# Value copies and the attention residual moved from ScalarE to VectorE, in an adapter, attention and mixture-of-experts kernel

## What is computed

```python
# layer 0: adapter with an expert chosen per sequence, then a norm
x = layer_norm(up(expert(gelu(down(x)))) + x)
# layer 1: attention (16 heads of 16 features) and a feed-forward net
x = ln(x) * (1 + scale) + shift             # scale, shift per sequence, from the timestep
q, k, v = x @ Wq + bq, x @ Wk + bk, x @ Wv + bv
probs = softmax(mask(q @ k.T / 4 + attention_bias))
x = x + ((probs @ v) @ Wo + bo)             # the residual of this case
x = x + gelu2((ln(x) * g2 + beta2) @ W1 + b1) @ W2 + b2
# layer 2: pairs of features rotated by theta and phi of the sequence
# layer 3: norms, a style, then each token through 2 of 8 experts of width 1024
y = sum(gate[e] * (relu(h @ w1[e] + b1[e]) @ w2[e] + b2[e]) for e in top2(softmax(h @ router)))
out = x + y
```

## Time and profile before

| | us |
|---|---|
| median of 3 runs | 693.06 |
| lowest and highest run | 692.5 and 694.13 |
| the profiled execution | 692.5 |
| its span in the trace | 690.7 |
| TensorE busy (matmuls) | 553.9 (80%) |
| VectorE busy | 470.9 (68%) |
| ScalarE busy | 289.4 (42%) |
| GpSimd busy | 259.1 (38%) |

### The profile page before, as it was taken

The page is one execution under the profiler, slowest core; times in us unless marked ns, Lnnn a source line. Parts: engine busy times, 40 slices in busy tenths (PEclk is TensorE's granted clock), DMA queues, the critical chain, the costliest instruction groups (busy, mean ns, idle before and its releaser), DMA issues.

```text
span 690.7 us, 15770 instructions
## 1 busy us (share of the span) xinstructions
PE 553.9 (80%) x5032; PEld 414.4 (60%) x5033; DVE 470.9 (68%) x1284; ACT 289.4 (42%) x596; POOL 259.1 (38%) x161
## 2 busy tenths in 40 slices
PE   2618587999588798778966499999989999999992
PEld 1505365676466385663855347767767777777771
DVE  5581797799969979972699662886653646474651
ACT  1313643734444325345333241666464435353540
POOL 0723554718506636125771140212441313132222
PEclk9557779999898989989988689999999999999996
DMA  8623445303024433308424685783632322222220
GB/s 293 225 91 122 153 147 195 132 1 123 35 89 159 178 132 112 123 25 312 152 93 145 238 318 189 282 273 55 156 75 45 48 35 48 33 46 38 44 42 0
DMA packets 41177, 86.37 MB, mean 125 GB/s; under 512 B 7321, under 2 KB 31938, under 8 KB 37026
## 3 DMA queue, kind: packets, MB, share of 16 engines
q1 hardware_dynamic: 22896, 65.16, 26.9%
q0 software_dynamic: 7200, 8.60, 7.5%
q10 hardware_dynamic: 11026, 11.89, 5.7%
HBM read 57.10 MB, written 29.44 MB: 125 GB/s over the span
## 4 chain that ended last, share of the span: by engine, by line
PE 51%; DVE 26%; DMA 6%; issue 6%; ACT 5%; ACTq 2%; POOL 2%; SPq 0%; DVEq 0%; POOLq 0%
PE bank L1902 8%; PE bank L1727 6%; PE bank L1891 5%; PE bank L1736 4%; PE bank L1893 4%; PE bank L1892 4%; PE bank L1903 4%; DMA out_x<-x_kept,ids 4%; PE bank L1624 2%; PE bank L1691 2%; DMA stage<-in_moe_w 2%; PE bank L1707 2%; DVE stats L1040 2%; PE bank L1611 2%; DVE w_moe L1151 2%
## 5 line engine op out<-in xcount | busy, mean ns | idle before, releaser
L1891 PE MATMUL bank<-xs_f,w_moe 128*128 128x128 f16 x624 | 123.2, 221 | 13.4 <-ACT stage L869 6.1
L653 POOL DMA_INDIRECT out_x<-x_kept,ids x39 | 61.6, 1579 | 167.3 <-DVE x_kept L1493 98.0
L1893 PE MATMUL bank<-xs_f,w_moe 128*128 128x128 f16 x624 | 123.4, 221 | 0.0
L1892 PE MATMUL bank<-xs_f,w_moe 128*128 128x128 f16 x624 | 122.8, 220 | 0.0
L869 ACT ACTIVATE stage<-bank,cols 128x128 f32<-128x128 f32 x312 | 88.4, 375 | 79.9 <-PE bank L1893 39.0
L1891 PEld LDWEIGHTS bank<-xs_f,w_moe 128*128 x624 | 61.1, 98 | 50.4 <-issue 21.9
L1902 PE MATMUL bank<-w_moe,split 128*128 x208 | 79.3, 383 | 0.4
L605 POOL DMA_INDIRECT dispatched<-disp,slot x32 | 35.9, 1121 | 97.8 <-DVE disp L1251 54.5
L1007 DVE SCALAR_TENSOR_TENSOR split<-stage,split 128x2048 f16<-128x2048 f32 x16 | 42.4, 2650 | 34.3 <-ACT split L692 34.3
L1727 PE MATMUL bank<-w_moe 128*128 128x512 f32 x128 | 60.6, 634 | 3.1 <-ACT w_moe L753 3.1
L1892 PEld LDWEIGHTS bank<-xs_f,w_moe 128*128 x624 | 61.4, 98 | 2.8
(11 more groups left out here) (271 smaller groups left out, 1210.3 us busy)
## 6 DMA issues: line engine op xcount, KB each, us to landing
stage<-in_moe_w SPq DMA_DIRECT2D x16, 1024.0 KB, 8.5
w_split<-split SPq DMA_DIRECT2D x16, 1024.0 KB, 4.9
w_moe<-w_split SPq DMA_DIRECT2D x8, 2048.0 KB
w_moe<-in_bias SPq DMA_DIRECT2D x8, 1024.0 KB, 10.0
xs<-dispatched ACTq DMA_DIRECT2D x41, 130.0 KB
w_moe<-in_x_f SPq DMA_DIRECT2D x4, 512.0 KB, 5.9
w_moe<-in_x_t SPq DMA_DIRECT2D x4, 512.0 KB, 4.6
out_x<-x4b ACTq DMA_DIRECT2D x4, 512.0 KB, 3.6
```

The lines of the kernel that those rows point to most:

```text
L653: pool.indirect_dma_start(out=out[:, :], out_offset=bass.IndirectOffsetOnAxis(ap=ids[m][:, 0:1], axis=0), in_=ys[j], in_offset=None, bound ...
L1891: pe.matmul(o, hi, xs_f[j][:, k, :], start=(k == 0), stop=False)
L1892: pe.matmul(o, hi, xs_f[j][:, KD + k, :], start=False, stop=False)
L1893: mm = pe.matmul(o, lo, xs_f[j][:, k, :], start=False, stop=(k == KD - 1))
```

## The change

Four edits. The copy of bank 1 to `v_bd` moves from ScalarE to VectorE (`values` in both blocks; ScalarE keeps bank 0). `take_x2` leaves ScalarE; VectorE's new `residual` adds `bo`, now laid out as a row over all partitions, while it takes banks 6 and 7 to `x2`. `keep` no longer adds `bo` and is one instruction of 128 x 1024. And the parameter load of `b2` (128 KB) becomes one of `bo` and `b2` together (256 KB).

```diff
-            (b2, t["b2"].broadcast_to([P, D])), (w1, t["w1"].rearrange("(k p) n -> p k n", p=P)),
+            (biases, t["biases"].broadcast_to([P, 2, D])), (w1, t["w1"].rearrange("(k p) n -> p k n", p=P)),
...
             def values(c):
 
-                for half, ready in enumerate((v0_ready, v1_ready)):
-                    act.wait_ge(v_done.sem, v_done.of(c, half + 1))
-                    for s in range(2):
-                        act.activation(
-                            v_bd[64 * s:64 * s + 64, 4 * half:4 * half + 4, :, s, :].rearrange("p b j d -> p (b j) d"),
-                            bank[half][64 * s:64 * s + 64, :].rearrange("p (j d) -> p j d", d=HD),
-                            ACT.Copy).then_inc(ready.sem, 1)
+                act.wait_ge(v_done.sem, v_done.of(c, 1))
+                for s in range(2):
+                    act.activation(v_bd[64 * s:64 * s + 64, 0:4, :, s, :].rearrange("p b j d -> p (b j) d"),
+                                   bank[0][64 * s:64 * s + 64, :].rearrange("p (j d) -> p j d", d=HD),
+                                   ACT.Copy).then_inc(v0_ready.sem, 1)
 
             def keep(c):
 
                 act.wait_ge(x1_ready.sem, x1_ready.of(c, 2))
                 act.wait_ge(wo_done.sem, wo_done.of(c, 0))
-                for k in range(KD):
-                    ins = act.activation(x1_kept[:, k, :], x1[:, k, :], ACT.Identity, bias=bo[:, k:k + 1])
-                ins.then_inc(kept_ready.sem, 1)
-
-            def take_x2(c):
-
-                for g in range(2):
-                    act.wait_ge(wo_done.sem, wo_done.of(c, g + 1))
-                    act.activation(x2[:, 2 * g:2 * g + 2, :], bank[6 + g][:].rearrange("p (n d) -> p n d", d=D),
-                                   ACT.Copy).then_inc(x2_ready.sem, 1)
+                act.activation(x1_kept[:], x1[:], ACT.Copy).then_inc(kept_ready.sem, 1)
...
+                def values():
+
+                    dve.wait_ge(v_done.sem, v_done.of(c, 2))
+                    for s in range(2):
+                        dve.tensor_copy(v_bd[64 * s:64 * s + 64, 4:8, :, s, :].rearrange("p b j d -> p (b j) d"),
+                                        bank[1][64 * s:64 * s + 64, :].rearrange("p (j d) -> p j d", d=HD)
+                                        ).then_inc(v1_ready.sem, 1)
...
+                def residual():
+                    for g in range(2):
+                        dve.wait_ge(wo_done.sem, wo_done.of(c, g + 1))
+                        dve.tensor_tensor(x2[:, 2 * g:2 * g + 2, :], bank[6 + g][:].rearrange("p (n d) -> p n d", d=D),
+                                          bo[:].unsqueeze(1).broadcast_to([P, 2, D]), ALU.add).then_inc(x2_ready.sem, 1)
...
             split_low(0, 0)
+            values()
             scores(0)
...
             norms()
             stages = second_half(0)
-            norm2, *_ = stages
+            residual, norm2, *_ = stages
+            residual()
             scale_norm, *_ = attention(1)
             scale_norm()
             split_low(0, 3)
```

More of the change, by code:

```diff
@@ L174, in build @@
         iota_p, parity, freqs, angle, down_b = (col[n] for n in ("iota_p", "parity", "freqs", "angles", "down_b"))
-        b_ada, bq, bk, bv, bo, b1 = (col[n] for n in ("b_ada", "bq", "bk", "bv", "bo", "b1"))
+        b_ada, bq, bk, bv, b1 = (col[n] for n in ("b_ada", "bq", "bk", "bv", "b1"))
         g2, beta2, ln_g, ln_b = (col[n] for n in ("g2", "beta2", "ln_g", "ln_b"))
@@ L818, in _ @@
             context(0, 1)
-            take_x2(0)
             split_high(0, 3)
@@ L844, in _ @@
                 context(c + 1, 1)
-                take_x2(c + 1)
                 split_high(c + 1, 2)
@@ L1122, in sums @@
                         finish()
-                return scale_norm, scores, sums
+                return scale_norm, values, scores, sums
             def second_half(c):
                 vec, _ = stepper(second_step, c)
+                def residual():
[3 more added lines that the diff above has]
+                                          bo[:].unsqueeze(1).broadcast_to([P, 2, D]), ALU.add).then_inc(x2_ready.sem, 1)
                 def norm2():
@@ L1267, in accumulate @@
                                                  x4[:, 2 * g:2 * g + 2, :], ALU.mult, ALU.add).then_inc(acc_ready.sem, 1)
-                return (norm2, second_residual, rotate, norm3, style_stats, style_scale, style_apply, choose,
+                return (residual, norm2, second_residual, rotate, norm3, style_stats, style_scale, style_apply, choose,
                         token_gates, find_place, copy_gates, accumulate, fill_rows)
             hidden, residual, norms = adapter(0)
-            scale_norm, scores, sums = attention(0)
+            scale_norm, values, scores, sums = attention(0)
             step(dve.tensor_copy(time_f[:], time_i[:]))
@@ L1364, in _ @@
             for c in range(NCH - 1):
-                _, scores, sums = attention(c + 1)
-                (_, second_residual, rotate, norm3, style_stats, style_scale, style_apply, choose,
+                _, values, scores, sums = attention(c + 1)
+                (_, _, second_residual, rotate, norm3, style_stats, style_scale, style_apply, choose,
                  token_gates, find_place, copy_gates, accumulate, fill_rows) = stages
+                values()
                 if c + 2 < NCH:
@@ L2062 @@
         "w_ada": a["L1_cond_W_ada"], "w_qkv": np.concatenate([a["L1_cond_Wq"], a["L1_cond_Wk"], wv], 1),
-        "wo": a["L1_cond_Wo"], "b2": row(a["L1_cond_b2"]),
+        "wo": a["L1_cond_Wo"], "biases": np.stack([a["L1_cond_bo"], a["L1_cond_b2"]])[None],
         "w1": a["L1_cond_W1"], "w2": a["L1_cond_W2"], "subj_emb": a["L3_cond_subj_emb"],
```

9 lines of the change are left out of this document (5 added, 4 removed).

## The result

The changed kernel takes 698.55 us (median of 11 runs, 696.46 to 700.35), the kernel before on the same chip 693.84 (11 runs, 691.72 to 695.92). The ratio is 1.0075, with a 95% interval of 1.006 to 1.0089: slower by 4 to 6 us. The sign was forecast; the time, 696.1 with a range of 692.8 to 698.2, was too low.

A forecast was written before the change was run, and what follows sets the result against it. No engine is full; in the attention stage the chain of waits hops between engines. 0.15 + 2.8 + 0.1 = +3.05 us on 692.5 gave 695.55 for such an execution, 696.1 for the median; range 692.8 to 698.2.

The forecast's parts named there:

- The sign: Whole kernel: slower at 0.68, same at 0.27, faster at 0.05.
- Values on VectorE: Values copies moved to VectorE: +0.15 us in chunk 0, +0.1 in chunk 2, nothing in chunks 1 and 3.
- `x2` in chunks 1 to 3: VectorE's two additions of 0.68 us fit into its idle before the routing choice: zero.
- in chunk 0, +0.1: x2 additions between the norms and scale_norm of chunk 1: the second ends at 112.37, scale_norm began at 112.23; +0.1 us.
- The collision: VectorE's low split goes ahead of GpSimd's second shift half in chunk 1; queries start at 117.4 instead of 115.09, +2.3 us.
- The clock: TensorE's idle before chunk 1's queries grows to 4.9 us, its clock falls to 1.2 GHz: 1.6 us lost (0 to 2.1).
- What of it passes: Of TensorE's 3.9 us, +2.8 goes on: VectorE reads chunk 1's first score at 150.25 instead of 147.46.
- Behind it all is relative: After chunk 1's scores and rotation the +2.8 us goes on; weight loads, too, are issued when VectorE has split.
- last rival: TensorE also falls to the lower clock later, or mask additions shift into more small VectorE steps: 698.5 us; chance 0.10.
- a difference arising after 170 us: Check on the new profile: if the difference arises after 170 us, its reason is another than the forecast's.

The follow-up runs named there:

- values_only: The kernel before, with only the copy of the values' second bank moved to VectorE: 693.39 us, ratio 1.0.
- late_split: The changed kernel, with ScalarE waiting for both halves of x2 of chunk 0 before split_high(0, 3): 693.74 us, ratio 1.0017.
- warm_gap_short: early_split plus four matmuls with unused results on TensorE ahead of the queries of chunk 1: 696.87 us, ratio 1.0056.
- warm_turn3_short: early_split plus four matmuls with unused results ahead of the transposes of chunk 1 in the loop: 696.13 us, ratio 1.005.
- two_waits: The changed kernel, with VectorE waiting for both halves of GpSimd's shift before its low split, in chunks 0 and 1: 693.39 us, ratio 0.9986.
- early_split: The kernel before, with ScalarE doing split_high(0, 3) ahead of take_x2(0), nothing moved between engines: 699.5 us, ratio 1.0082.
- warm_gap: early_split plus nine matmuls with unused results on TensorE ahead of the queries of chunk 1: 698.57 us, ratio 1.0071.
- wait_for_shift: The changed kernel, with VectorE waiting for both halves of GpSimd's shift of chunk 1 before split_low(0, 3): 695.06 us, ratio 1.0025.
- warm_turn3: early_split plus seven matmuls with unused results ahead of the transposes of chunk 1 in the loop: 698.1 us, ratio 1.0053.
- warm_both: early_split plus four unused matmuls at each of two places, ahead of chunk 1's queries and its transposes in the loop: 695.94 us, ratio 1.0038.
- warm_before: The kernel before, with matmuls with unused results in TensorE's idle stretches of the attention stage: 687.17 us, ratio 0.9919.
- warm_before_wait: The kernel before, with VectorE's wait for the shift in chunk 0 and unused matmuls in TensorE's idle stretches: 683.14 us, ratio 0.9865.

## Why the prediction was right in sign and wrong in size

Step by step, distances taken as in the table.

- *Values on VectorE, +0.15 and +0.1.* Their size cannot be told from nothing: `values_only` has a ratio of 1.0, `late_split` holds every moved copy and is at +0.1 in the trace. At the place itself, VectorE ended its first four additions 4.10 us behind TensorE's first score instead of 3.90, +0.2. Two readings were off: the earlier trace rows does show a float32 copy out of a bank (L1206, 128x32 in 0.19 us), only too small to price this one; and in chunk 2, 1.2 us less a wait of 0.95 leaves 0.25, not 0.1. The copy itself took more than I set: 1.41 us for two, 0.70 each, the value of the additions and not one between them and the float16 copy.

```profile
67.56 1.41 DVE L1098 COPY w_moe<-bank 64x512 f32<-64x512 f32 x2 [13.37 <-PE bank L1648]
```

  The Trainium skill ("VectorE: DVE Perf Modes", "Why PSUM operands drop a tier") says that a float32 operand in PSUM leaves VectorE at 1x. The row agrees; the prediction had read only the tier table of that page, whose general bound of 2x is for any type.
- *`x2` in chunks 1 to 3, zero; in chunk 0, +0.1.* Right. In the loop the second addition waits for TensorE, as in `300.02 0.69 DVE L1129` of the changed kernel, idle 1.93 us ahead of it.
- *The collision, +2.3 with the 0.1.* Right: the queries start 5.71 us behind the transposes instead of 3.59, +2.12.
- *The clock, +1.6.* Right: 8.68 instead of 7.13, +1.55. TensorE was then 3.67 us late (its turn at 131.62 less 110.81, against 128.64 less 111.50); forecast 3.9.
- *What of it passes, +2.8.* Right: VectorE read the first score of chunk 1 at 149.30, idle for TensorE, 38.49 us behind the transposes instead of 35.96, +2.53; at the third turn of chunk 0 the same +2.5. The mechanism was the forecast one: the steps of the root that GpSimd's masks had stretched to 1.19 us now took 0.16.

```profile
137.75 0.16 DVE L1018 TENSOR_TENSOR newton<-newton,var 128x4 f32<-128x4 f32 x1
...
149.30 2.48 DVE L1108 TENSOR_TENSOR w_moe<-bank,w_moe 128x512 f32<-128x512 f32 x4 [1.87 <-PE bank L1669]
```

- *"Behind it all is relative".* This is the step that failed. The 2.6 us arrive at 283 unchanged, and then TensorE loses 1.9 us at the lower clock in the transposes, contexts and products from 286 to 293 us, and 1.4 in the feed-forward net of chunk 3 (17.03 us against 15.59 for its 32 matmuls). The first expert tile is 5.8 us late. The term on the clock was thus counted once, with 1.6, where the trace has it three times, with 4.9 us in all. The first two losses are tied to the change by experiments (`late_split`, `warm_gap_short`, `warm_turn3_short`). The third is not: the kernel before idles the same 5.24 us there and has its transposes at 1.97 us too, only its clock comes back sooner. It does not grow with the lateness either (16.93 us in `two_waits`, 0.9 late; 15.84 in `warm_turn3_short`, 3.0 late), and the profiled execution of the changed kernel, with its stall ahead of it, had 15.59. What decides it stays open. The prediction had this as its last rival ("the late TensorE also falls to the lower clock later"), at 0.10 and 698.5. That this is the measured figure is in part luck: its 2.4 us above the forecast are two more steps of VectorE's root at 1.2 each, which did not come (seven of about 1.19 us between 232 and 245 us in the kernel before and in both traces of the changed one), and the two later losses of clock are 3.3. The range ended 0.35 us below the result. It had also said that a difference arising after 170 us would have another reason than the forecast's; more than half of it arose there.

How a delay of TensorE makes its clock fall 165 us later can be seen in the idle ahead of the third turn of chunk 1. In the kernel before, the context of chunk 2 ran at the lower clock and so ended late, close to the release of the turn by VectorE, and the idle was short:

```profile
272.13 1.06 PE L1681 MATMUL bank<-mats,w_moe 128*128 128x128 f32 x8 [2.70 <-ACT w_moe L706]
273.91 1.96 PE L1681 MATMUL bank<-mats,w_moe 128*128 128x128 f32 x8 [0.71 <-ACT w_moe L743]
275.79 3.89 PE L1691 MATMUL bank<-w_moe 128*32 128x64 f32 x64
282.76 1.09 PE L1589 MATMUL bank<-mats,w_moe 128*128 128x128 f32 x8 [3.08 <-DVE w_moe L1050]
```

In `early_split` the same context ran at the upper clock, TensorE ended it only 1.1 us late instead of 2.6, idled 4.56 us, and the clock fell there, ahead of work on the chain:

```profile
275.84 1.06 PE L1681 MATMUL bank<-mats,w_moe 128*128 128x128 f32 x8 [2.18 <-ACT w_moe L706]
277.62 1.14 PE L1681 MATMUL bank<-mats,w_moe 128*128 128x128 f32 x8 [0.71 <-ACT w_moe L743]
278.69 3.18 PE L1691 MATMUL bank<-w_moe 128*32 128x64 f32 x64
286.43 1.97 PE L1589 MATMUL bank<-mats,w_moe 128*128 128x128 f32 x8 [4.56 <-DVE w_moe L1050]
```

So, in the kernel before, a fall of the clock in work that was hidden kept the idle behind it short. `warm_turn3_short` shows that the fall behind the longer idle is the cause of the step from +2.6 to +4.5: with the clock held at this one place it does not appear. `warm_gap` shows that the lateness alone is not: it was 3.3 us late there, its context ran at the lower clock (5.85 us for its last two rows, as in the kernel before), the idle was 3.06, the clock stayed up, and the ranking was still 3.3 late. What goes along with the two outcomes is the idle ahead of the context (the first row of each fence). In the six traces where it was 2.60 to 2.75 us (`before`, `late_split`, `values_only`, `wait_for_shift`, `two_waits`, `warm_gap`) the clock fell in the context; in the seven where it was 1.61 to 2.47 (both of the changed kernel, `early_split`, `warm_turn3`, `warm_gap_short`, `warm_turn3_short`, `warm_both`) it did not. This is a match in the traces, and no run varied that idle alone. Not shown is why `wait_for_shift`, only 0.3 us late there, loses 0.9 us at 286 us as well. The Trainium skill ("TensorE: Matmul & The Clock Gate", "What's actually happening") says that the gate's watch runs free of the program, so that the same kernel has more or fewer slow matmuls from run to run; the 8.60 and 10.15 us of the first queries in two executions of the changed kernel agree.

## What to carry to other kernels

Where the busiest engine waits for others again and again, a delay is not carried on as it is: it changes the idle stretches behind it, and the clock can fall in another of them than before. So price a delay at every later idle of similar length, not at the first alone. And look first at work that starts earlier by the change: here the cost came from an instruction that nobody had touched, two queues away, and an order wait (one line, `late_split`) takes it back. Last, idle stretches of the tensor engine on the chain can be filled with matmuls that nobody reads; here that was worth 9 to 11 us together with the wait in chunk 0, and 4.8 on the kernel before as it was, as long as they end ahead of the release.

## What had not been expected of the hardware

- The clock at the same place of the same code is not fixed: 16 matmuls behind an idle of 4.35 us took from 8.54 to 10.15 us in eleven kernels, and 8.60 and 10.15 in two executions of one of them.
- A collision of VectorE and GpSimd that stretches a 1.05 us addition to 3.10 costs the total between nothing and about 2 us by itself in this kernel; with the falls of the clock that came with it, 5 to 6.
- Taking the same collision out of chunk 0 started the queries 2.2 us earlier, and 1.7 us of it reached the end (`two_waits` against `wait_for_shift`). With the clock held the same wait made 4.0 us between `warm_before` and `warm_before_wait`, of which the overrun shown above may be up to 2.6.
- Whether the clock fell in a context went with the idle ahead of it, 2.60 to 2.75 us or 1.61 to 2.47, and where it did not fall there, it fell behind the next idle, of 4.02 to 4.59 us, unless that was filled.
